# Nine chunks per pass of the attention loop, and half of the k projection before the last y

## The chip, the cores and the metric

The kernel runs on one core of a Trainium2 chip. The metric is device time in microseconds (us) from start to end of the program; the median of several runs counts. The core has five engines that run side by side and wait for each other by semaphores: PE (TensorE, matrix products), DVE (VectorE), ACT (ScalarE), POOL (GpSimd) and SP (SyncE, which issues the DMAs here). Each engine works through its own list of instructions strictly in order.

## What is computed

The reference is one block of a model on x of 2 x 4096 tokens with 512 channels: modulated layer norm, an RWKV-6 attention, a gated residual, a second layer norm and a feed-forward net whose operands are quantised to FP4. The attention, cut to its core:

```python
sx = concatenate([zeros_like(x[:, :1]), x[:, :-1]], axis=1) - x
m = tanh((x + sx * time_maa_x) @ tm_w1).reshape(Bb, Tt, 5, A)
mix = time_maa_wkvrg[None, None] + einsum('btfa,fac->btfc', m, tm_w2)
xw, xk, xv, xr, xg = [x + sx * mix[:, :, i] for i in range(5)]
r, k, v, g = xr @ Wr, xk @ Wk, xv @ Wv, silu(xg @ Wg)
w = exp(-exp(time_decay + tanh(xw @ td_w1) @ td_w2))
def step(state, rkvw):          # over the tokens, for each head
    a = k_t[..., :, None] * v_t[..., None, :]
    y = einsum('bhk,bhkv->bhv', r_t, state + u[None, :, :, None] * a)
    return w_t[..., :, None] * state + a, y
```

Then y is normalised per head, multiplied by g and projected by Wo. Neither the mathematics nor the number of operations is touched by the change.

## The kernel before

The program has two stages, one after the other: `attention` writes x1 to memory, `feed_forward` reads it. Only `attention` is changed.

`attention` cuts the 4096 tokens into 32 chunks of 128 (both sequences together, `ni` = 32) and runs a software pipeline over them. Each engine has a body (`pe_body`, `dve_body`, `act_body`, `pool_body`, `sp_body`), which `run` writes out for iterations 0, 1 and 2, then once inside a hardware loop (`eng.Fori(3, ni - 2)`, iterations 3 to 29, so 27 passes and 26 jumps back), and then for 30 to 33 again. In iteration i a body does three things for three chunks: the projections of chunk i (flag `do_p`), the scan over the tokens of chunk c = i - 1 (`do_w`), and the output projection of chunk f = i - 2 (`do_f`); with `more` it also prepares chunk i + 1.

An iteration has two parts.

- The **scan part**. For each of the 8 sub-blocks n (2 sequences x 4 stretches of 32 tokens) PE computes scores (`pe_scores`, lines 403 to 414, 128 small products in the trace), DVE turns them into the matrix Am and the new state (`dve_A`, L846, L853, L859, L875), and PE multiplies them into y (`pe_y`, L429 and L432, into the bank `YB`). Between them stand the mixing products `pe_delta` (L461), their use on DVE (L743), the decay (L472, L480) and the output projection (L504). The first scores, n = 0, are issued at the very end of the iteration before, so the jump of the loop stands between scores 0 and the first `pe_delta`. The scan ends with `dve_ww` (L755), which copies the decay out of the two banks `PROJ`, then `dve_A` of n = 7, and `pe_y` of n = 7.
- The **tail**. PE transposes the next chunk (`pe_x`, L441), then does the projections k, r (L493), the small product `pe_tm1` (L449), the projections v and g, and the scores 0 of this chunk. A projection fills the two `PROJ` banks half by half (h = 0, 1). Before each half PE waits until the bank's former content is gone: `ww_done` for k, `k_done` for r, `ru_done` for v, `vT_done` for g. ACT copies out k (`act_k`, L611) and r (`act_r`, L615 to L621), and also copies y (`act_yT`, L575), shifts and scales the transposed chunk (`act_hT`, L545, L550) and computes the decay (`act_w`, L597, L600; `act_fg`, L606, L607). DVE computes factors from the decay (L763 to L782), transposes y (L882), makes the token difference (L724, L728), derives scaled k's (L790 to L795) and r's (L806 to L824), transposes v (L828) and k (L833), and ends with the statistics of the chunk after next (L710 to L718).

The order on each engine is that of the bodies as written; no scheduler moves anything. Waits are on semaphore values that depend on the iteration, so in the loop they are made in registers (`after`, `settled_then`).

Of the kernel before, what the change touches and what calls it, by code (L numbers as in the profile page):

```python
# [17 lines left out]


# [1 line left out]

# [68 lines left out]
def after(eng, signal, chunk, k=None):  # L90

    value = signal.at(chunk, k)
    if not isinstance(value, int) or value > 0:
        eng.wait_ge(signal.sem, value)
# [40 lines left out]
def attention(nc, x1, x, maa_x, maa, tm_w1, tm_w2, decay, td_w1, td_w2, faaaa, Wr, Wk, Wv, Wg, Wo,  # L135
              ln_w, ln_b, c_in, wmod, ident_in, diag_in, pick_in, ni=NI):
    with ExitStack() as ctx:
# [5 lines left out]
        def sig(name, per, step=1):  # L143
            return Signal(ctx, nc, name, per, step)
# [195 lines left out]
        ww_done = sig("ww_done", 1)  # L340
# [124 lines left out]
        def xf_wait(eng, i, j):  # L465
            after(eng, xf_done_v, i) if j == 0 else after(eng, xf_done_p, i, j)
# [9 lines left out]
        def pe_td2(pe, i):  # L476
            after(pe, u1_done, i)
            after(pe, mixed, i)
            for g in range(G):
                last = nc.tensor.matmul(PROJ[g // 2][:, (g % 2) * BT:(g % 2 + 1) * BT], w_td2[:, g * P:(g + 1) * P], u1[:],  # L480
                                        start=True, stop=True)
            last.then_inc(td2_done.sem, 1)

        def pe_proj(pe, i, j, free):
            f = ORDER[j]
            xf_wait(pe, i, j)
            buf = xf[:, j % NXF]
            w = {MIX_K: w_k, MIX_R: w_r, MIX_V: w_v, MIX_G: w_g}[f]
            for h in range(2):
                free(h)  # L490
                for g in (2 * h, 2 * h + 1):
                    for k in range(G):
                        last = nc.tensor.matmul(PROJ[h][:, (g % 2) * BT:(g % 2 + 1) * BT], w[:, k, g * P:(g + 1) * P],  # L493
                                                buf[:, k].rearrange("p b t -> p (b t)"), start=(k == 0), stop=(k == G - 1))
                last.then_inc(proj_done.sem, 1)
# [11 lines left out]
        def pe_body(pe, i, do_p, do_w, do_f, more, more2):  # L507
            c, f = i - 1, i - 2
            for n in range(1, 8):
                if n == 1 and do_p:  # L510
                    pe_delta(pe, i, 0)
                if do_w:
                    pe_scores(pe, c, n)
                    pe_y(pe, c, n - 1)
                if n == 2 and do_p:
                    pe_td1(pe, i)
                if 2 <= n <= 5 and do_p:
                    pe_delta(pe, i, n - 1)
                if n == 3 and do_f:
                    pe_wo(pe, f, 0, do_p)  # L520
                if n == 5 and do_f:
                    pe_wo(pe, f, 1, do_p)
                if n == 6 and do_p:
                    pe_td2(pe, i)
            if do_w:
                pe_y(pe, c, 7)
            if more:
                pe_x(pe, i + 1)
            if do_p:
                pe_proj(pe, i, 1, lambda h: after(pe, ww_done, i))  # L530
                pe_proj(pe, i, 2, lambda h: after(pe, k_done, i, h + 1))
            if more:
                pe_tm1(pe, i + 1)
            if do_p:
                pe_proj(pe, i, 3, lambda h: after(pe, ru_done, i, h + 1))
                pe_proj(pe, i, 4, lambda h: after(pe, vT_done, i, h + 1))
                pe_scores(pe, i, 0)
# [34 lines left out]
        def act_yT(act, c, b):  # L572
            after(act, y_done, c, 4 * b + 4)
            after(act, yS_done, c - 1)
            nc.scalar.activation(yT[:, :, b, :], YB[:].rearrange("p (g t) -> p g t", g=G), ACT.Copy).then_inc(yT_done.sem, 1)  # L575
# [19 lines left out]
        def act_w(act, i):  # L595
            after(act, ww_done, i)
            nc.scalar.activation(flat4(wexp), flat4(wexp), ACT.Exp).then_inc(wexp_done.sem, 1)  # L597
            after(act, wexp_done, i)
            after(act, der, i - 1)
            nc.scalar.activation(flat4(wT), flat4(wexp), ACT.Exp, scale=-1.0).then_inc(w_done.sem, 1)  # L600

        def act_fg(act, i):
            after(act, w_done, i)
            after(act, derk, i - 1)
            w4 = wT[:].rearrange("p g b (x e) -> p (g b x) e", e=4)
            nc.scalar.activation(F4[:, :, 1:2], w4[:, :, 0:1], ACT.Copy)  # L606
            nc.scalar.activation(G4[:, :, 2:3], w4[:, :, 3:4], ACT.Copy).then_inc(fg_done.sem, 1)  # L607

        def act_k(act, i, h):
            after(act, proj_done, i, h + 1)  # L610
            nc.scalar.activation(kvar[:, 0, 2 * h:2 * h + 2].rearrange("p g b t -> p (g b t)"), PROJ[h][:], ACT.Copy).then_inc(k_done.sem, 1)  # L611
# [32 lines left out]
        def act_body(act, i, do_p, do_w, do_f, more, more2):  # L644
            c, f = i - 1, i - 2
            if do_p:
                after(act, td1_done, i)
                after(act, td2_done, c)
                nc.scalar.activation(u1[0:D_RANK, :], SMALL[0:D_RANK, 0:BT], ACT.Tanh).then_inc(u1_done.sem, 1)
            if more:  # L650
                act_xn(act, i + 1)
            if do_w:
                act_yT(act, c, 0)
            if do_p:
                act_w(act, i)
            if do_w:
                act_yT(act, c, 1)
            if do_p:
                act_fg(act, i)
            if more:  # L660
                act_hT(act, i + 1)
            if do_w:
                act_square(act, c)
            if do_p:
                act_k(act, i, 0)
                act_k(act, i, 1)
                act_r(act, i, 0)
                act_r(act, i, 1)
                act_k32(act, i)
                act_m1(act, i)  # L670
            if more:
                act_m(act, i + 1)
            if more:
                act_stack(act, i + 1)
            if do_p:
                act_gu(act, i, 0)
                act_gu(act, i, 1)
            if do_w:
                act_affine(act, c)
# [270 lines left out]
        def run(eng, body):  # L950
            body(eng, 0, True, False, False, True, True)
            body(eng, 1, True, True, False, True, True)
            body(eng, 2, True, True, True, True, True)
            with eng.Fori(3, ni - 2) as i:
                body(eng, i, True, True, True, True, True)
            body(eng, ni - 2, True, True, True, True, False)
            body(eng, ni - 1, True, True, True, False, False)
            body(eng, ni, False, True, True, False, False)
            body(eng, ni + 1, False, False, True, False, False)
# [658 lines left out]
```

## Time and profile before

| | us |
|---|---|
| median of 3 runs | 4909.59 |
| lowest, highest | 4905.96, 4915.21 |
| the profiled execution's own time | 4901.52 |
| span from its first to its last instruction | 4899.7 |
| end of the attention in that span, about | 2940 |

The trace lists each instruction with its start and length on its engine, and in square brackets how long the engine sat idle before it and who ended that wait. "issue" as the releaser means that nothing recorded in the profile held the instruction back. Times are from the start of the span. A matrix product in fp32 shows as two records. PE's weight loads are a row of their own, beside PE.

### The profile page before, as it was taken

How to read it: one execution, taken by the hardware profiler on the slowest of the kernel's cores; microseconds unless marked ns; L12 is line 12 of the kernel's file. 1: busy time of each engine (PE TensorE's matmuls, PEld its weight loads, DVE VectorE, ACT ScalarE, POOL GpSimd, SP SyncE). 2: the span in 40 equal slices, each digit the busy share in tenths (PEclk: the TensorE clock that was granted, in tenths of full speed). 3: DMA queues.
4: the chain of work that ended last, by engine and by line, in shares of the span. 5: the costliest groups of instructions: out<-in, count | busy, mean ns of one | idle time of the engine just before them, and what ended most of it. 6: DMA issues, size and time to landing. Idle time of an engine off the chain costs nothing. (4 is left out here: it accounts for less than half of the span.)

```text
span 4899.7 us, 152762 instructions
## 1 busy us (share of the span) xinstructions
PE 4014.8 (82%) x64712; PEld 2745.0 (56%) x64712; DVE 3835.3 (78%) x7929; ACT 1368.0 (28%) x2555; POOL 1387.7 (28%) x735
## 2 busy tenths in 40 slices
PE   5888888888888878888888861499899989989998
PEld 3666666666666766666667651244444444444444
DVE  4676776766767767667677748699999999999997
ACT  2333243332332423323324212212122221212221
POOL 1111211111112111111121113444444444444443
PEclk7888898887988889889889875699999999999999
DMA  3000000000000000000000002001010010101000
GB/s 99 13 27 16 20 24 16 29 16 20 24 16 24 20 16 29 16 20 24 16 25 20 12 24 89 22 20 32 26 32 31 27 32 26 32 26 32 30 28 26
DMA packets 72819, 131.50 MB, mean 27 GB/s; under 512 B 12705, under 2 KB 13473, under 8 KB 72290
## 3 DMA queue, kind: packets, MB, share of 16 engines
q1 hardware_dynamic: 72290, 123.00, 7.9%
q8 instruction: 508, 8.32, 0.7%
q14 instruction: 21, 0.17, 0.0%
HBM read 89.43 MB, written 33.55 MB: 25 GB/s over the span
## 5 line engine op out<-in xcount | busy, mean ns | idle before, releaser
L693 POOL TENSOR_TENSOR xf<-xf,hT 128x1024 f32<-128x1024 f32 x128 | 278.2, 2174 | 1555.1 <-DVE xf L743 1555.1
L859 DVE COPY_PREDICATED Am<-pick,banks 128x64 f32<-128x64 uint8 (+2 forms) x1792 | 460.5, 257 | 121.7 <-DVE Am L859 6.4
L1505 PE MATMUL fbank<-gT,xqT 128*128 128x464 f16 (+1 forms) x2304 | 536.0, 387 | 16.0 <-DVE h L1364 13.8
L1505 PE MATMUL fbank<-uT,xqT 128*128 128x464 f16 (+1 forms) x2304 | 487.7, 361 | 0.0
L1527 PE MATMUL fbank<-dT,hqT 128*128 128x512 f16 x2112 | 476.8, 379 | 0.2 <-ACT hqT L1440 0.2
L704 POOL TENSOR_TENSOR yrs<-yvar,neg_half 128x32 f32<-128x32 f32 x32 | 203.1, 6346 | 789.8 <-DVE yvar L888 789.8
L1505 PEld LDWEIGHTS fbank<-gT,xqT 128*128 128x128 f16 x2304 | 236.6, 104 | 275.8 <-issue 57.0
L1454 ACT ACTIVATE sil<-fbank,und 128x464 f32<-128x464 f32 (+1 forms) x192 | 125.2, 652 | 912.1 <-PE fbank L1505 912.1
L429 PE MATMUL banks<-Am,v_s 32*32 32x32 f32 x8192 | 228.2, 210 | 182.3 <-DVE Am L859 92.2
L1505 PEld LDWEIGHTS fbank<-uT,xqT 128*128 128x128 f16 x2304 | 225.6, 98 | 231.6 <-issue 1.2
L743 DVE SCALAR_TENSOR_TENSOR xf<-banks,col_maa,sx 128x256 f32<-128x256 f32 x640 | 265.0, 477 | 104.2 <-PE banks L461 104.2
L846 DVE TENSOR_TENSOR Am<-banks,diag 128x128 f32<-128x128 f32 x256 | 74.0, 289 | 346.5 <-PE banks L414 344.8
L1321 POOL TENSOR_TENSOR hq<-q16h,s16h 128x1408 f16<-128x1408 f16 x64 | 210.4, 3288 | 443.6 <-DVE s16h L1311 443.6
L1527 PEld LDWEIGHTS fbank<-dT,hqT 128*128 128x128 f16 x2112 | 201.4, 98 | 220.2 <-issue 1.0
L429 PEld LDWEIGHTS banks<-Am,v_s 32*32 32x32 f32 x8192 | 191.6, 121 | 202.7 <-issue 195.6
L403 PE MATMUL banks<-rcol,kvar 32*32 32x80 f32 x8192 | 247.9, 261 | 52.5 <-issue 52.5
L569 ACT ACTIVATE m_stack<-xxx 32x256 fp32r<-32x256 f32 x640 | 265.0, 414 | 75.8 <-DVE xxx L734 58.8
L407 PE MATMUL banks<-rcol,kvar 32*32 32x48 f32 x8192 | 240.5, 223 | 36.3 <-issue 35.9
L403 PEld LDWEIGHTS banks<-rcol,kvar 32*32 32x32 f32 x8192 | 185.6, 121 | 145.2 <-issue 137.2
L853 DVE TENSOR_TENSOR s_tmp<-state,T 128x128 f32<-128x128 f32 x256 | 254.7, 995 | 0.0
L409 PE MATMUL banks<-rcol,kvar 32*32 32x16 f32 x8192 | 226.1, 188 | 33.6 <-issue 33.5
L504 PE MATMUL banks<-w_o,yn 128*128 128x512 f32 x512 | 238.4, 610 | 17.7 <-DVE yn L899 16.9
(230 smaller groups left out, 8995.6 us busy)
## 6 DMA issues: line engine op xcount, KB each, us to landing
x_tok<-in_L_attn_x SPq DMA_DIRECT2D x32, 512.0 KB, 4.0
xres<-in_L_attn_x SPq DMA_DIRECT2D x32, 512.0 KB, 3.9
x_after_attention<-xres SPq DMA_DIRECT2D x32, 512.0 KB, 3.5
xl<-x_after_attention SPq DMA_DIRECT2D x64, 256.0 KB, 2.7
xr<-x_after_attention SPq DMA_DIRECT2D x64, 256.0 KB, 2.7
out<-xr SPq DMA_DIRECT2D x64, 256.0 KB, 2.1
raw_g<-in_L_wmod SPq DMA_DIRECT2D x3, 1024.0 KB, 5.5
raw_g<-in_L_ffn_w_gate SPq DMA_DIRECT2D x1, 2816.0 KB, 10.9
```

Of the source, the lines that this page charges most:

```text
L403: nc.tensor.matmul(sc[d, g * NS:(g + 1) * NS], kvar[d, 0, g, b, 32 * q:32 * q + 32], rcol[d, X, 0:M1], start=True, stop=True)
L407: nc.tensor.matmul(scm[d, g * NM:g * NM + X0 - M1], kvar[d, 1, g, b, 32 * q:32 * q + 32], rcol[d, X, M1:X0], start=True, stop=True)
L409: nc.tensor.matmul(scm[d, g * NM + X0 - M1:(g + 1) * NM], kvar[d, 2, g, b, 32 * q:32 * q + 32], rcol[d, X, X0:SEND], start=True, stop=True)
L429: nc.tensor.matmul(out, v_s[d, g, b, q, :], Am[d, n % 2, g, :], start=True, stop=False)
L504: last = nc.tensor.matmul(SMALL[:], yn[:, k, b, :], w_o[:, b, k, :], start=(k == 0), stop=(k == G - 1))
L569: last = nc.scalar.activation(m_stack[A_RANK * part:A_RANK * (part + 1), j, :], m_part[part % 2][src, f // 4, :], ACT.Copy)
L693: nc.gpsimd.tensor_tensor(xf[:, j % NXF].rearrange("p g b t -> p (g b) t"), xf[:, j % NXF].rearrange("p g b t -> p (g b) t"), hT[:, :, :, ...
L743: last = nc.vector.scalar_tensor_tensor(xf[:, j % NXF, g], PROJ[g // 2][:, (g % 2) * BT:(g % 2 + 1) * BT].rearrange("p (b t) -> p b t", b= ...
L853: nc.vector.tensor_tensor(s_tmp[:], state[:, b, q], t32, ALU.mult).then_inc(s_step.sem, 1)
L859: nc.vector.copy_predicated(dst, mask, src).then_inc((done or A_step).sem, 1)
L1505: last = nc.tensor.matmul(GU[2 * pair + t][:, 0:w], xqT[:, u, a, g, :], W[:, b_, g, lo_:hi_], start=(k == 0), stop=(k == 3 * G - 1))
L1527: last = nc.tensor.matmul(DN[1 - u][:], hqT[:, a, kk, :], dT[:, b_, kk, :], start=(k == 0), stop=(k == 3 * KF - 1))
```

## The change

Three edits.

1. The loop's body now holds nine iterations: `per = gcd(ni - 5, 9)` is 9, and the loop runs 3 times (`lap`) with the iteration number `per * lap + 3 + k`. Two jumps back are left of 26. All five engines are written this way.
2. On PE the first half of the k projection (h = 0) moves from behind `pe_x` to in front of `pe_y(c, 7)`, with its waits: for the mixed input and for `ww_done`.
3. On ACT `act_fg` and the copy of that half, `act_k(i, 0)`, move in front of the second `act_yT`.

```diff
-        def pe_proj(pe, i, j, free):
+        def pe_proj(pe, i, j, free, halves=(0, 1)):
...
-            for h in range(2):
+            for h in halves:
...
+            if do_p:
+                pe_proj(pe, i, 1, lambda h: after(pe, ww_done, i), (0,))
             if do_w:
                 pe_y(pe, c, 7)
             if more:
                 pe_x(pe, i + 1)
             if do_p:
-                pe_proj(pe, i, 1, lambda h: after(pe, ww_done, i))
+                pe_proj(pe, i, 1, lambda h: after(pe, ww_done, i), (1,))
                 pe_proj(pe, i, 2, lambda h: after(pe, k_done, i, h + 1))
...
             if do_p:
                 act_w(act, i)
+            if do_p:
+                act_fg(act, i)
+                act_k(act, i, 0)
             if do_w:
                 act_yT(act, c, 1)
-            if do_p:
-                act_fg(act, i)
             if more:
                 act_hT(act, i + 1)
             if do_w:
                 act_square(act, c)
             if do_p:
-                act_k(act, i, 0)
                 act_k(act, i, 1)
...
-            with eng.Fori(3, ni - 2) as i:
-                body(eng, i, True, True, True, True, True)
+            per = math.gcd(ni - 5, 9)
+            with eng.Fori(0, (ni - 5) // per) as lap:
+                for k in range(per):
+                    body(eng, per * lap + (3 + k), True, True, True, True, True)
```

PE at the end of an iteration in the loop, before: the last of the scores 0, then the loop's count and jump.

```order
L407 MATMUL banks<-rcol,kvar 32x48 x4
L409 MATMUL banks<-rcol,kvar 32x16 x4
L414 MATMUL banks<-v_s,kT 32x32 x16
L954 REGISTER_ALU
L954 COMPARE_AND_BRANCH
```

The same place after, between two of the nine iterations (L462 is the first `pe_delta`).

```order
L410 MATMUL banks<-rcol,kvar 32x16 x4
L415 MATMUL banks<-v_s,kT 32x32 x16
L95 ISA
L462 MATMUL banks<-m_stack,w_tm 128x256 x4
L404 MATMUL banks<-rcol,kvar 32x80 x16
```

The jump is gone; `pe_delta` follows the scores directly.

PE from the last y to the r projection, before (L429 and L432 are the end of y 7, L441 the transposes).

```order
L429 MATMUL banks<-Am,v_s 32x32 x4
L432 MATMUL banks<-r,state 32x32 x4
L94 REGISTER_ALU
L441 MATMUL banks<-ident,xn 128x128 x8
L94 ISA
L493 MATMUL banks<-xf,w_k 128x256 x16
```

The same after; L430 and L433 are the y products, those above L494 of y 6 and those below of y 7.

```order
L433 MATMUL banks<-r,state 32x32 x4
L95 ISA
L494 MATMUL banks<-xf,w_k 128x256 x8
L114 REGISTER_ALU
L430 MATMUL banks<-Am,v_s 32x32 x4
...
L433 MATMUL banks<-r,state 32x32 x4
L95 REGISTER_ALU
L442 MATMUL banks<-ident,xn 128x128 x8
L494 MATMUL banks<-xf,w_k 128x256 x8
```

Eight of the sixteen k products now stand ahead of y 7.

ACT from the decay to the copies of k, before.

```order
L600 ACTIVATE wT<-xxx 128x1024
L94 REGISTER_ALU
L575 ACTIVATE yT<-banks 128x4x128
L94 ISA
L606 ACTIVATE F<-wT 128x256
L607 ACTIVATE G<-wT 128x256
L94 ISA x2
L545 ACTIVATE hT<-hT 128x8
```

The same after.

```order
L603 ACTIVATE wT<-xxx 128x1024
L95 ISA
L609 ACTIVATE F<-wT 128x256
L610 ACTIVATE G<-wT 128x256
L95 ISA
L614 ACTIVATE kvar<-banks 128x512
L95 REGISTER_ALU
L578 ACTIVATE yT<-banks 128x4x128
L95 ISA x2
L548 ACTIVATE hT<-hT 128x8
```

The copy of k's first half, L614, has come in front of the copy of y, L578; the other copy of k stays behind the transposed chunk.

## Rows read from the trace of the kernel before

**Rows 1.** The page, busy time of each engine, share of the span, instructions.

```profile
PE 4014.8 (82%) x64712; PEld 2745.0 (56%) x64712; DVE 3835.3 (78%) x7929; ACT 1368.0 (28%) x2555; POOL 1387.7 (28%) x735
```

**Rows 2.** Windows: stretch, length, busy time by engine, PE clock, DMA share, GB/s.

```profile
387.79:2698.22 2310.43, 1924.34 (x45240) 1540.88 (x45241) 1647.39 (x3953) 771.62 (x1639) 414.75 (x182) 0.87 0.07 21
304.95:387.79 82.84, 73.07 (x1740) 58.84 (x1740) 61.01 (x152) 29.70 (x64) 15.94 (x7) 0.88 0.07 22
220.44:304.95 84.51, 71.82 (x1741) 56.91 (x1742) 61.50 (x153) 29.87 (x64) 15.95 (x7) 0.88 0.07 22
2698.22:2783.43 85.21, 73.88 (x1741) 59.14 (x1742) 59.84 (x146) 29.71 (x64) 15.94 (x7) 0.88 0.05 15
```

**Rows 3.** Timeline of DVE around a jump back: start, us, operation, idle before.

```profile
1541.81 0.29 DVE L846 TENSOR_TENSOR Am<-banks,diag 128x128 f32<-128x128 f32 x1 [2.61 <-PE banks L414]
...
1543.93 0.70 DVE L859 COPY_PREDICATED Am<-pick,banks 128x64 f32<-128x64 uint8 x2
1550.98 0.29 DVE L846 TENSOR_TENSOR Am<-banks,diag 128x128 f32<-128x128 f32 x1 [6.36 <-PE banks L414]
```

**Rows 4.** Timeline of PE around the same jump.

```profile
1541.17 0.45 PE L414 MATMUL banks<-v_s,kT 32*32 32x32 f32 x32
1545.45 0.73 PE L461 MATMUL banks<-m_stack,w_tm 128*128 128x256 f32 x4 [3.82 <-issue]
...
1548.18 1.14 PE L403 MATMUL banks<-rcol,kvar 32*32 32x80 f32 x26 [1.66 <-issue]
```

**Rows 5.** Waits of PE from 387.7 to 2698.3: total us, times, longest.

```profile
PE banks L461 <- issue: 103.1, 26, 4.4
```

**Rows 6.** Timeline of DVE at two iteration starts without a jump.

```profile
223.88 0.29 DVE L846 TENSOR_TENSOR Am<-banks,diag 128x128 f32<-128x128 f32 x1 [0.99 <-PE banks L414]
...
225.70 0.62 DVE L859 COPY_PREDICATED Am<-pick,banks 128x64 f32<-128x64 uint8 x2
...
304.95 0.29 DVE L846 TENSOR_TENSOR Am<-banks,diag 128x128 f32<-128x128 f32 x1 [2.69 <-PE banks L414]
...
307.65 0.29 DVE L846 TENSOR_TENSOR Am<-banks,diag 128x128 f32<-128x128 f32 x1
```

**Rows 7.** DMA queues, 387 to 476, then 300 to 387: packets, MB, share.

```profile
q8 instruction: 16, 0.26, 1.2%
...
q8 instruction: 14, 0.23, 1.2%
q14 instruction: 3, 0.02, 0.1%
```

**Rows 8.** Timeline of PE in a tail, from the last y.

```profile
1501.15 0.24 PE L432 MATMUL banks<-r,state 32*32 32x32 f32 x6
1505.21 0.57 PE L429 MATMUL banks<-Am,v_s 32*32 32x32 f32 x7 [3.82 <-DVE Am L859]
...
1508.28 7.28 PE L493 MATMUL banks<-xf,w_k 128*128 128x256 f32 x32
1515.39 7.07 PE L493 MATMUL banks<-xf,w_r 128*128 128x256 f32 x32
```

**Rows 9.** Timeline of DVE in the same tail.

```profile
1500.99 1.21 DVE L755 TENSOR_SCALAR xxx<-banks 128x1024 f32<-128x1024 f32 x1
...
1512.67 1.67 DVE L728 SCALAR_TENSOR_TENSOR xxx<-sx,col_maax,hT 128x256 f32<-128x256 f32 x4
1516.22 1.23 DVE L790 TENSOR_TENSOR kvar<-kvar,G 128x1024 f32<-128x1024 f32 x1 [1.88 <-ACT kvar L611]
```

**Rows 10.** Windows of the same tail, columns as in rows 2.

```profile
1506.00:1508.00 2.00, 2.00 (x48) 1.94 (x39) 1.90 (x5) 1.38 (x3) 0.00 (x0) 0.50 0.70 247
1508.00:1541.70 33.70, 33.62 (x275) 28.33 (x273) 23.80 (x42) 22.19 (x53) 6.35 (x1) 0.99 0.01 1
```

**Rows 11.** Timelines of PE and DVE in the second iteration written out.

```profile
252.73 5.22 PE L504 MATMUL banks<-w_o,yn 128*128 128x512 f32 x8
...
259.57 0.29 DVE L846 TENSOR_TENSOR Am<-banks,diag 128x128 f32<-128x128 f32 x1 [4.27 <-PE banks L414]
```

More of the change, by code:

```diff
@@ L20 @@
 from contextlib import ExitStack
+import math
 import concourse.bass as bass
```

## The prediction

> **What bounds the kernel now.** The page comes first. Over the span PE is busy 82% and DVE 78% [rows 1], so neither is full and the two take turns waiting. The change touches only the attention, so I looked for the length of one of its iterations. I took the start of `dve_A` of n = 0 (L846) as the mark. From the first start after a jump to the first start behind the loop are 26 iterations: 2310.43 / 26 = 88.86 us each [rows 2]. Three further iterations of the same shape have no jump ahead of their scan: the first pass of the loop, 82.84 us, and two that are written out, 84.51 and 85.21 us [rows 2]. The reader sees here already that an iteration behind a jump costs 3.7 to 6.0 us more.
>
> The timelines show where. In the loop DVE starts `dve_A` of n = 0 at 1541.81, is done with it at 1544.63, and then sits idle 6.36 us until the scores of n = 1 arrive at 1550.98 [rows 3]. From mark to mark that is 9.17 us. PE had ended the scores 0 at 1541.62 and stood still 3.82 us before the next product and 1.66 us more among the scores, both for "issue", nothing that the profile shows as a semaphore [rows 4]. Not one case but all: 26 such stops before L461, together 103.1 us, 4.0 each [rows 5]. The instruction queue of PE agrees: 16 blocks were fetched in an iteration behind a jump, 14 in the one without [rows 7]. Without a jump the same distance from n = 0 to n = 1 is 307.65 - 304.95 = 2.70 us, or 223.88 - 220.44 = 3.44 us [rows 2, 6].
>
> The tail is bound by PE. It is busy 33.62 of 33.70 us, at a clock of 0.99 [rows 10]. Right before that stretch it stands idle 3.82 us, because y 7 waits for Am of n = 7 [rows 8]. DVE then waits for what PE makes: 1.88 us for k [rows 9], and at the tail's end 2.61 us for scores 0 [rows 3].
>
> **Edit 1, nine iterations a pass.** It removes 24 of 26 jumps. From the rows the gross gain at one boundary is 9.17 - 2.70 = 6.47 us. Part is given back, since the scan that follows without a jump is not as smooth: whole iterations without one are only 6.0, 4.4 and 3.7 us shorter than 88.86 [rows 2]. One reason is visible: in the second of them the output projection L504 took 5.22 us, and DVE waited 4.27 us for the scores behind it [rows 11]. The first pass of the loop, 82.84, is the one that has exactly the loop's code, with waits made in registers; the other two have constants there. So the sum takes 5.0 us, between the 6.0 of the exact code and the mean 4.1 of the other two: 24 x 5.0 = 120 us. The high bound is the whole gap, 24 x 6.47 = 155 us. The low bound is an estimate: a `dve_A` in a written-out iteration took 226.32 - 223.88 = 2.44 us [rows 6] against 1544.63 - 1541.81 = 2.82 in the loop [rows 3], since its waits are made with constants. Eight times 0.38 is 3.0 of the 4.1, so 1.1 would be left, 24 x 1.1 = 26 us. The bodies have no more register steps than before (79 for each iteration on DVE by the order of the instructions, 82 before), so no wait becomes dearer.
>
> On what causes such a stop the Trainium skill bears ("Runtime: NRT & Kernel Launch", section "Instruction fetch mechanics"). It says that a taken branch to a target outside the fetched window waits for a DMA of the target, and that streaming straight code is mostly hidden. By the first statement the trace agrees, with 4.0 us a jump. By the second the full 155 us would be gained; the 84.51 and 85.21 speak against taking it whole. Another page ("Advanced Engine Details and Errata", section "Control Flow Timing") puts a compare-and-branch at about 108 ns; by it alone 24 jumps would be worth 2.6 us, which the 3.82 us stops contradict.
>
> **Edit 2, half of the k projection ahead of y 7.** PE stops at 1501.39 and `ww_done` comes at 1502.20 [rows 8, 9]. The half costs 7.28 / 2 = 3.64 us and ends at 1505.84 instead of leaving PE idle until 1505.21. So y 7 starts 0.63 us late. y 7 and the transposes take 1508.28 - 1505.21 = 3.07, to 1508.91; the other half takes 3.64, to 1512.55. Before, k ended at 1515.39, when r began [rows 8]. Everything behind it on PE comes 2.84 us earlier, if nothing else becomes late.
>
> What could be late next? DVE's token difference waits for the transposes, 0.63 us later now, so `xxx`, which ended at 1512.67 + 1.67 = 1514.34, ends at 1514.97 at the latest [rows 9]. PE wants it for `pe_tm1`, which now comes at 1519.6: 4.6 us to spare. DVE's k work can start at once, since k was ready for it 1516.22 - 1515.39 = 0.83 us after PE's end of k [rows 8, 9], which makes 1513.38; the 1.88 us of waiting vanishes and DVE is 1.25 us ahead of before. It then meets r, 2.84 us ahead, where it is 1.6 us behind PE's gain; before, it waited there too, so at most 0.4 us of that shows, and each later wait of DVE in the tail was for PE too. At the end it had 2.61 us in hand [rows 3]. So PE still sets the end. The saving counts in iterations 1 to 31, the ones with both a scan and projections: 31 x 2.8 = 87 us. In iteration 0 there is no y 7 and nothing is won.
>
> Bounds: y 7 and the transposes ran at a clock of 0.50 after the idle time [rows 10]. If the half fills that gap and the clock stays up, up to 0.8 us more is won, 3.6 in all, or 112 us. If instead the half itself runs at half clock, it takes 7.28, y 7 starts at 1509.5 and k ends at 1516.2, which is 0.8 us later than before: a loss of 25 us. PE works until 1501.39 at full length just before [rows 8], so the value near full clock is taken.
>
> **Edit 3, ACT's order.** `act_fg` needs nothing but the decay. It fills ACT's wait for y 7 and costs nothing. The copy of k's first half costs 0.83 us at most, by the same difference as above; it waits for PE's half at 1505.84 and ends at 1506.67, while y 7 starts at 1505.84 and is the next thing ACT waits for. So it hides too, but for a few tenths. If the half is slow, the copy of y waits behind it, but y 7 on PE stands behind the same half, so no new delay arises.
>
> **The sum.** 4901.5 - 120 - 87 = 4694.5 for an execution like the profiled one. The median of the runs shown lies 8.1 us above that execution, so 4702.6; I give 4702.
>
> **Rivals.**
> - *Streaming gives most back.* Nine different iterations lie at other block boundaries and other phases of the clock, and stops like that of rows 11 take most of the gain: 26 + 87 = 113 us, time 4797. For it: 85.21. Against: the first pass, 82.84.
> - *The tail gains nothing.* The half runs at low clock, or DVE becomes the one that is waited for. The gain is 120 us, time 4790. For it: the 0.50 [rows 10]. Against: DVE's 2.61 us in hand.
> - *All of it.* Straight code streams without a stop and the clock stays up: 155 + 112 = 267 us, time 4643. The Trainium skill's "mostly hidden" (the page and section named above) would give this side of it, the 155.
> - *Slower.* Before, the short lists of DVE, ACT and POOL stay inside and are not fetched again in the loop; the queue q14 moved 3 blocks in the first pass and none in the next window [rows 7]. Now DVE streams as well. If DVE itself stops for a block, nothing covers it in the scan, where each step hangs on it. At 4.0 us a stop as for PE, two in an iteration, 8.0, cost what both edits bring (5.0 + 2.8), and from there on the change loses. Three in each of 24 give 24 x (12.0 - 7.8) = 100 us, 5010. Against it: the iterations written out already stream on DVE, and all of DVE's waits there end with PE or ACT.
> - *Nothing happens* would need the loop to jump as often as before. The instruction order rules that out, with nine bodies between two jumps.
>
> **How the numbers follow.** Forecast 0.70, streaming gives back 0.12, tail gains nothing 0.09, all of it 0.05, slower 0.03, nothing measurable 0.01. The range runs from just above the full gain to just beyond the two weak cases, 4650 to 4805. It leaves out the full gain, the slower case and nothing, about 0.09, and about as much again for sizes beyond the bounds. A change within 0.2% (10 us) is about what a measurement of this kernel cannot tell from none. Faster 0.96, same 0.01, slower 0.03.
>
> **What would show it.** In the trace after: from mark to mark 88.9 - 5.0 - 2.8, about 81 us within a lap, and 86 behind the two jumps left. The stops before the first `pe_delta` gone but for two. Fourteen blocks for PE in an iteration. The idle time before y 7 near 0.8 us and in front of the half, not behind it. From `ww_done` to the next `dve_A` of n = 0 36.8 us instead of 1541.81 - 1502.20 = 39.6. DVE still idle before scores 0. I am wrong if DVE shows stops for issue, if the whole scan has PE stops of 2 to 3 us that DVE waits for, or if the half of k takes 7 us.

## The result and the profile after

The changed kernel takes 4743.6 us (median of 4 runs, 4739.1 to 4748.5) against 4912.4 us before; the ratio is 0.9658, 95% interval 0.9641 to 0.9675. That is 169 us less, where 207 were forecast. The profiled execution has a span of 4739.7 us against 4899.7, so 160.0 us less, and its parts say where they come from.

The page of the kernel after, busy time as in [rows 1]:

```profile
PE 3970.0 (84%) x64712; PEld 2691.6 (57%) x64712; DVE 3788.9 (80%) x7929; ACT 1375.0 (29%) x2555; POOL 1388.1 (29%) x735
```

The windows of the kernel after. The first row is the 26 iterations that answer to the first of [rows 2]; the second is one tail that ran well (in the first pass of the loop, ahead of the 26), the third one that did not.

```profile
383.87:2548.83 2164.96, 1888.05 (x45240) 1497.98 (x45240) 1597.15 (x3952) 778.16 (x1639) 411.68 (x182) 0.89 0.07 22
348.53:383.87 35.34, 35.11 (x345) 29.55 (x346) 28.66 (x59) 26.18 (x57) 6.35 (x1) 1.00 0.10 30
1421.84:1463.55 41.71, 38.45 (x409) 32.11 (x410) 28.84 (x58) 25.95 (x57) 6.35 (x1) 0.92 0.08 25
```

The 26 iterations went from 2310.4 to 2165.0 us, which is 145.5 of the 160.0. One iteration is 83.27 us long on the mean instead of 88.86. The rest is in the iterations ahead of them, about 4 us, and in those written out behind the loop, about 11, which have the moved half of k too. The feed-forward stage did not change: from the last output of the attention on DVE to the end it is 1964 us in both.

The boundary between two iterations, timeline of DVE after (compare [rows 3]):

```profile
383.87 0.29 DVE L849 TENSOR_TENSOR Am<-banks,diag 128x128 f32<-128x128 f32 x1 [2.50 <-PE banks L415]
...
386.76 0.29 DVE L849 TENSOR_TENSOR Am<-banks,diag 128x128 f32<-128x128 f32 x1
```

and of PE (compare [rows 4]):

```profile
383.35 0.45 PE L415 MATMUL banks<-v_s,kT 32*32 32x32 f32 x32
383.73 0.75 PE L462 MATMUL banks<-m_stack,w_tm 128*128 128x256 f32 x4
```

`pe_delta` follows the scores with no stop, and DVE goes from n = 0 to n = 1 in 2.89 us instead of 9.17. The waits of PE over the 26 iterations (compare [rows 5]):

```profile
PE banks L433 <- issue: 86.6, 48, 3.6
PE banks L430 <- issue: 60.1, 35, 3.3
...
PE banks L462 <- issue: 7.4, 2, 3.7
```

Two lines of the same view before, both for the y products:

```profile
PE banks L429 <- DVE Am L859: 83.0, 28, 3.8
PE banks L429 <- issue: 71.9, 69, 2.6
```

The stops before the first `pe_delta` are gone but for two, those of the two jumps left. But others have appeared: PE now stops inside the y products (L430, L433), 147 us in all. Before, L429, the same line as L430 here, had 72 us of them and L432 none. The first of the two lines is the gap ahead of y 7 that edit 2 was to fill, 3.2 us an iteration; after, PE waits for Am only 2.5 us in all.

The tail that ran well, timeline of PE (compare [rows 8]):

```profile
348.76 3.81 PE L494 MATMUL banks<-xf,w_k 128*128 128x256 f32 x16 [0.95 <-DVE xxx L758]
352.50 0.26 PE L430 MATMUL banks<-Am,v_s 32*32 32x32 f32 x8
...
353.20 1.07 PE L442 MATMUL banks<-ident,xn 128*128 128x128 f32 x8
354.11 3.62 PE L494 MATMUL banks<-xf,w_k 128*128 128x256 f32 x16
357.57 7.07 PE L494 MATMUL banks<-xf,w_r 128*128 128x256 f32 x32
```

The half of k stands in the former gap; PE idles 0.95 us ahead of it and not at all behind. From the start of y 7 to the second half of k it takes 1.61 us instead of 3.07, at a clock of 1.00, where it was 0.50 before [rows 10]. This stretch is as short in all of the 26 iterations. The idle time ahead of the half is not: there PE waits for the decay only once, 0.5 us. Otherwise it arrives late, since it has stood for issue before, and the half starts 2.3 us after the decay is copied out on the mean. The tail that ran badly, the same engine:

```profile
1425.70 0.26 PE L430 MATMUL banks<-Am,v_s 32*32 32x32 f32 x2 [3.25 <-issue]
1426.05 6.20 PE L494 MATMUL banks<-xf,w_k 128*128 128x256 f32 x16
1432.88 1.07 PE L442 MATMUL banks<-ident,xn 128*128 128x128 f32 x8
```

Here PE stopped 3.25 us for issue inside y 6, after which the half of k ran at low clock and took 6.20 us. The clock from 1426.05 to 1432.25 was 0.59. The tail is 41.71 us long, longer than any of the 26 in the kernel before. Over the 26 the half takes 4.75 us on the mean, 3.7 in eight of them and 6.2 to 6.5 in five, and the tails last from 35.6 to 41.7 us.

To see where an iteration gained and lost I took, for each kernel, the starts of the eight `dve_A` (the line L846 or L849) of the 26 iterations, and averaged the distances. All tables below are made that way.

| us, mean of 26 iterations | before | after | difference |
|---|---|---|---|
| n = 0 to 1 (behind the jump) | 9.57 | 3.80 | -5.77 |
| n = 1 to 7 (the scan) | 39.24 | 41.74 | +2.50 |
| n = 7 to the next 0 (the tail) | 40.05 | 37.73 | -2.32 |
| iteration | 88.86 | 83.27 | -5.59 |

The first and the last row of differences came about as forecast in kind. The middle one is the surprise: the scan gives back 2.5 us an iteration, 65 us in all. Most of it is in two steps: n = 5 to 6 takes 8.31 us instead of 6.16, and n = 3 to 4 takes 7.27 instead of 6.44. From n = 1 to 7 DVE now stands idle 8.3 us an iteration instead of 4.0, nearly always for PE, while its own work there takes 30.3 us instead of 32.1; why the latter is less stays open.

### The profile page after: what moved, and what is told of

Read it like the earlier page. It is cut to its first block and busy times, and to the rows that moved or that the text cites. A ratio compares the mean times of both kernels' runs of the same rounds, so it can differ in the third digit from the quotient of the medians.

```text
span 4739.7 us, 152203 instructions
## 1 busy us (share of the span) xinstructions
PE 3970.0 (84%) x64712; PEld 2691.6 (57%) x64712; DVE 3788.9 (80%) x7929; ACT 1375.0 (29%) x2555; POOL 1388.1 (29%) x735
## 5 line engine op out<-in xcount | busy, mean ns | idle before, releaser
L433 PE MATMUL banks<-r,state 32*32 32x32 f32 x8192 | 212.5, 204 | 103.8 <-issue 103.8
L849 DVE TENSOR_TENSOR Am<-banks,diag 128x128 f32<-128x128 f32 x256 | 74.1, 290 | 278.0 <-PE banks L415 276.6
L505 PE MATMUL banks<-w_o,yn 128*128 128x512 f32 x512 | 262.9, 662 | 21.4 <-DVE yn L902 16.9
L430 PE MATMUL banks<-Am,v_s 32*32 32x32 f32 x8192 | 209.0, 205 | 75.9 <-issue 69.9
L494 PE MATMUL banks<-xf,w_k 128*128 128x256 f32 x1024 | 266.0, 418 | 7.4 <-issue 4.5
L1494 PE MATMUL fbank<-ident,hq 128*128 128x128 f16 x1408 | 121.8, 247 | 150.1 <-POOL hq L1326 112.9
L408 PE MATMUL banks<-rcol,kvar 32*32 32x48 f32 x8192 | 219.1, 215 | 33.2 <-issue 33.1
L404 PE MATMUL banks<-rcol,kvar 32*32 32x80 f32 x8192 | 221.6, 246 | 28.4 <-issue 28.4
L410 PE MATMUL banks<-rcol,kvar 32*32 32x16 f32 x8192 | 208.5, 183 | 40.3 <-issue 40.3
```

The costliest lines, as they stand in the source:

```text
L404: nc.tensor.matmul(sc[d, g * NS:(g + 1) * NS], kvar[d, 0, g, b, 32 * q:32 * q + 32], rcol[d, X, 0:M1], start=True, stop=True)
L408: nc.tensor.matmul(scm[d, g * NM:g * NM + X0 - M1], kvar[d, 1, g, b, 32 * q:32 * q + 32], rcol[d, X, M1:X0], start=True, stop=True)
L433: last = nc.tensor.matmul(out, state[d, b, q, g, :], r32[d, X, :], start=False, stop=True)
L505: last = nc.tensor.matmul(SMALL[:], yn[:, k, b, :], w_o[:, b, k, :], start=(k == 0), stop=(k == G - 1))
```

## The experiments

### The two edits apart

`e1_unroll` is the changed kernel with the order of PE and ACT as before, so nine iterations a pass alone. The part of PE is shown; ACT's is that of `e3_act_old` below.

```diff
-            if do_p:
-                pe_proj(pe, i, 1, lambda h: after(pe, ww_done, i), (0,))
             if do_w:
                 pe_y(pe, c, 7)
             if more:
                 pe_x(pe, i + 1)
             if do_p:
-                pe_proj(pe, i, 1, lambda h: after(pe, ww_done, i), (1,))
+                pe_proj(pe, i, 1, lambda h: after(pe, ww_done, i))
```

> Nine iterations per pass, the k projection and ACT's order as before. Theory A (the two edits add up; the scan gives back 2.5 us an iteration because PE's instructions stream, whatever the tail does): the 24 jumps bring 6.2 us each at the start of the scan, minus 2.5 us in it, so 24 x 3.7 = 89 us, time 4823. The sum from n = 1 to n = 7 is about 41.7 us as in the changed kernel, against 39.2 before. Theory B (what is given back comes with the moved half of k, which shifts where PE's clock is low): the unrolling alone keeps 5.0 us or more per jump, time 4790 or less, and the stretch from n = 1 to n = 7 stays near 40 us.

`e2_khalf` is the changed kernel with one iteration a pass.

```diff
-            per = math.gcd(ni - 5, 9)
+            per = 1
```

> One iteration per pass as before, with the moved half of k and ACT's new order. Theory A (edits add up): the gain is the rest of the 169 us, some 75 to 80 us, time 4835; the tail is 37.5 us against 40.05. Theory B (the half brings its 2.8 us or more in every iteration and the loss lies in the combination): 31 x 2.8 = 87 us or more, time 4825 or less, tail 37 or less in every iteration, as the clock finds the same pattern each time.

| | us | ratio to before (95%) | n 0 to 1 | scan | tail | iteration |
|---|---|---|---|---|---|---|
| before | 4909.9 | | 9.57 | 39.24 | 40.05 | 88.86 |
| e1_unroll | 4828.2 | 0.9824 (0.9804 to 0.9844) | 3.88 | 42.17 | 39.92 | 85.98 |
| e2_khalf | 4825.6 | 0.9835 (0.9809 to 0.9860) | 9.62 | 39.42 | 37.07 | 86.11 |
| after | 4743.6 | 0.9658 (0.9641 to 0.9675) | 3.80 | 41.74 | 37.73 | 83.27 |

The edits add up: 82 + 84 = 166 us, against 169 together, within the intervals. The whole loss in the scan, 2.9 us, is there in `e1_unroll` without the moved half; in `e2_khalf` the scan is as before. There Theory A stands. In `e2_khalf` itself the time and the mean tail are nearer to what Theory B gave (4825 us and 37) than to Theory A's 4835 and 37.5, but not "in every iteration": its tails range from 35.8 to 39.8 us. So, as means of the 26 iterations, the unrolling brings 5.7 us at the boundary and pays 2.9 back. For each of the 24 jumps removed that is 3.1 us net by the 26 iterations of the trace (75 us), and 82 / 24 = 3.4 us by the medians. The moved half brings 3.0 us a tail on its own and 2.2 beside the unrolling.

### What ACT's order is worth

`e3_act_old` is the changed kernel with ACT as before: copy of y, then `act_fg`, then the transposed chunk, and only then both copies of k.

```diff
-            if do_p:
-                act_fg(act, i)
-                act_k(act, i, 0)
             if do_w:
                 act_yT(act, c, 1)
+            if do_p:
+                act_fg(act, i)
             if more:
                 act_hT(act, i + 1)
             if do_w:
                 act_square(act, c)
             if do_p:
+                act_k(act, i, 0)
                 act_k(act, i, 1)
```

> Nine iterations per pass and the half of k on PE ahead of y 7, but ACT's order as before (copy of y, then the decay factors, then both copies of k). If ACT's order hides as the prediction said, the time is that of the changed kernel within 10 us: the first copy of k is wanted only by r, 3.6 us later. If the order on ACT is needed, r waits for the copy of k behind the transposed chunk (about 358 instead of 353 in the trace, when k's second half ends at 357.6), up to 1 us an iteration, 30 us slower.

It took 4808.9 us (0.9784, 0.9763 to 0.9805), 65 us slower than the changed kernel. Its trace is of the longest of its four runs, 4827.9 us. The waits of PE over the 26 iterations:

```profile
PE banks L494 <- ACT kvar L614: 46.8, 26, 1.8
```

In every iteration the r projection stands 1.8 us, because its bank still holds the first half of k, which ACT copies only behind the transposed chunk. The tail is 40.04 us instead of 37.73, as long as before the change. I had expected at most 30 us. With it PE never waits for the copy of k, as the prediction said, but without it the edit on PE brings only about 20 us (4828.2 to 4808.9).

### The jumps left, and the length of a pass

`e4_per27` and `e5_per3` change one number each.

```diff
-            per = math.gcd(ni - 5, 9)
+            per = 27
```

> All 27 iterations in one pass, so no jump back at all; otherwise the changed kernel. If each jump costs what the two left show (8.83 and 9.31 us from n = 0 to n = 1 instead of 3.35), 2 x 5.7 = 11 us less, 4732, minus up to 5 us given back in the scan: 4732 to 4737. If a long stretch of code streams worse (its instructions are fetched once and never again), it is the same or slower than 4744.

```diff
-            per = math.gcd(ni - 5, 9)
+            per = 3
```

> Three iterations per pass: nine passes and eight jumps instead of two. By the run with the unrolling alone a jump removed is worth 82 / 24 = 3.4 us net, so six more cost 20 us: 4764. If instead the first few removed jumps bring most (the streaming loss grows with the length of the pass), it stays within 8 us of 4744.

With no jump at all it took 4748.3 us (0.9663, 0.9645 to 0.9682), the same as the changed kernel, where 7 to 12 us less were expected. Its trace shows where they went. The 26 iterations take 2155.1 us instead of 2165.0, so the last two jumps did bring 10 us. But the three iterations behind the loop, from n = 0 of the first to n = 7 of the last, take 209.7 us instead of 193.3, with the same code. With eight jumps it took 4790.8 us (0.9771, 0.9740 to 0.9803), 47 us more than with two, where I expected 20. Its timeline of DVE around a jump:

```profile
556.04 0.29 DVE L849 TENSOR_TENSOR Am<-banks,diag 128x128 f32<-128x128 f32 x1 [2.99 <-PE banks L415]
...
566.67 0.29 DVE L849 TENSOR_TENSOR Am<-banks,diag 128x128 f32<-128x128 f32 x1 [7.82 <-PE banks L415]
```

Of its 26 iterations the 8 behind a jump take 87.2 us and the other 18 take 83.0, so a jump costs 4.2 us net here; six of them are 25 us. The 26 iterations together took 2192.1 us, 27.1 more than after. The remaining 14 us of the spans' difference (4780.8 against 4739.7) are in the iterations ahead of the loop and behind it, whose code is the same in both: the three behind it take 203.4 us here and 193.3 in the changed kernel. `e2_khalf` and `e4_per27` have that code too and take 202.6 and 209.7, so the changed kernel's 193.3 is the exception, worth 9 to 16 us in its favour. Comparisons of nearly equal kernels by their total time turn on it. What sets it stays open; that it is the phase in which the code meets the clock and the instruction blocks is a guess.

### Is it the number of instructions, or PE's time?

The stops for issue in the scan suggest that PE waits for its instructions, of which a product in fp32 needs four: the trace shows two matmul records and two weight loads for each. (The "128 small products" of `pe_scores` named above are such matmul records, of 64 products.) Three runs change their number. `e6_dup_scan` issues the last 16 products of `pe_scores` twice for n = 2 to 5.

```diff
-            for g in range(G):
+            for g_ in range(2 * G if 2 <= n <= 5 else G):
+                g = g_ % G
                 for d in HEADS:
                     last = nc.tensor.matmul(sc[d, G * NS + g * K:G * NS + (g + 1) * K], kT[d, g, b, q, :], v_s[d, g, b, q, :], start=True, stop=True)
```

> The changed kernel with 16 small products (kT by v_s, the 32 x 32 ones behind each scores) issued twice for n = 2 to 5, with the same result: 256 more PE instructions in the scan of each iteration, one instruction block of 16 KB more, 4 x 0.45 = 1.8 us of PE time. Theory F (in the scan PE is held by the arrival of its instructions, about 3.8 us for each block): up to 3.8 us more an iteration, clearly more than the next run, 31 x 3 = 90 us or more. Theory C (only PE's own time and its clock count): most of the 1.8 us hides under DVE, 0 to 30 us slower than the changed kernel.

`e7_dup_tail` has the same edit with `5 * G if n == 0 else G`.

> The same 64 extra products an iteration, but all behind the scores of n = 0, at the end of the tail, where the rows show no block fetched for 20 us. PE's time there is on the path: 1.8 us an iteration, 32 x 1.8 = 58 us slower than the changed kernel under both theories. Theory F: less than the run with the extra products in the scan costs, or the same if the block that is drained here is missing at the scan's start. Theory C: more than the run in the scan, since nothing hides it here.

`e9_fewer` leaves the products L410 out for n = 2 to 5, so part of the scores is stale.

```diff
-                for d in HEADS:
+                for d in (() if 2 <= n <= 5 else HEADS):
                     nc.tensor.matmul(scm[d, g * NM + X0 - M1:(g + 1) * NM], kvar[d, 2, g, b, 32 * q:32 * q + 32], rcol[d, X, X0:SEND], start=True, stop=True)
```

> The changed kernel without the 16 products of 32 x 16 (L410) for n = 2 to 5; their columns of the scores are left stale, so part of the attention's result is missing. 256 PE instructions less in the scan, one block of 16 KB less, and about 4 x 0.3 us of PE time. Theory F: PE's stops in the scan (8 to 9 us an iteration for issue) shrink by 2 us or more and the iteration by 1 to 2, 30 to 60 us faster. Theory C: the iteration follows PE's own time at most, 0 to 20 us faster.

And two controls add time on PE with few instructions. `e10_time_scan`:

```diff
         def pe_wo(pe, f, b, fenced):
...
+            for _ in range(2 - b):
+                nc.tensor.matmul(SMALL[:], yn[:, 0, b, :], w_o[:, b, 0, :], start=True, stop=True)
```

> Control to the run with extra products in the scan: the changed kernel with three long products added (the first product of the output projection repeated, twice for b = 0 at n = 3 and once for b = 1 at n = 5, with the same result). By the rows 3 x 0.6 = 1.8 us of PE time at full clock as there, but 12 instructions instead of 256. Theory F (what counts in the scan is the number of PE instructions): much less than the 148 us there, 0 to 60 us slower than 4744. Theory C (PE's time): like that run, 100 us or more.

`e11_time_tail`:

```diff
         def pe_proj(pe, i, j, free, halves=(0, 1)):
...
+                for _ in range(4 if (j, h) == (4, 1) else 0):
+                    nc.tensor.matmul(PROJ[h][:, 0:BT], w[:, 0, 2 * h * P:(2 * h + 1) * P],
+                                     buf[:, 0].rearrange("p b t -> p (b t)"), start=True, stop=True)
```

> Control to the run with extra products in the tail: four products of the g projection repeated in each iteration, 4 x 0.455 = 1.8 us of PE time with 16 instructions instead of 256. PE's time is on the path there: 32 x 1.8 = 58 us under both theories. Theory F: the 119 us of the run with 256 short ones had some 60 us for their instructions. Theory C: 119 us here too.

The second control has the length that it was meant to have, 4 x 0.455 us. The first does not. The 0.6 us of its expectation are one of a product's two records. Four products of the output projection take 3.60 us at a clock of 1.00, so one takes 0.90, and three add 2.7 us and not 1.8:

```profile
500.19 3.60 PE L507 MATMUL banks<-w_o,yn 128*128 128x512 f32 x8
```

In the 26 iterations the added products, two records each, were busy 91.06 us on PE (first column behind the length), 3.50 us an iteration:

```profile
396.41:2638.08 2241.67, 91.06 (x156) 29.97 (x156) 0.90 0.07 21
```

| against after, 4743.6 us | added for an iteration | us | ratio to before (95%) | difference |
|---|---|---|---|---|
| e6_dup_scan | 256 instructions, 1.8 us of PE, in the scan | 4891.9 | 0.9967 (0.9954 to 0.9979) | +148 |
| e10_time_scan | 12 instructions, 2.7 us, in the scan | 4858.2 | 0.9891 (0.9859 to 0.9924) | +115 |
| e7_dup_tail | 256 instructions, 1.8 us, in the tail | 4863.0 | 0.9908 (0.9884 to 0.9931) | +119 |
| e11_time_tail | 16 instructions, 1.8 us, in the tail | 4808.6 | 0.9802 (0.9777 to 0.9828) | +65 |
| e9_fewer | 256 instructions less in the scan | 4649.7 | 0.9463 (0.9446 to 0.9479) | -94 |

Since the low clock stretches what is added, the windows of the 26 iterations compare better. In the order of the table (the changed kernel's row stands above), busy time of PE first:

```profile
395.82:2678.70 2282.88, 1960.51 (x48568) 1557.42 (x48569) 1541.48 (x3953) 778.01 (x1639) 411.46 (x182) 0.87 0.07 21
396.41:2638.08 2241.67, 1954.57 (x45397) 1524.20 (x45397) 1562.51 (x3953) 778.65 (x1639) 411.62 (x182) 0.90 0.07 21
403.90:2658.26 2254.36, 1949.52 (x48568) 1554.69 (x48568) 1597.17 (x3952) 777.75 (x1638) 411.92 (x182) 0.88 0.07 21
393.28:2595.58 2202.30, 1930.08 (x45449) 1532.91 (x45449) 1607.54 (x3952) 778.81 (x1639) 412.01 (x182) 0.90 0.07 22
380.72:2472.14 2091.42, 1854.37 (x41912) 1463.16 (x41913) 1541.23 (x3952) 779.08 (x1639) 415.92 (x182) 0.89 0.07 23
```

| us, mean of 26 iterations | iteration | PE busy | PE idle | idle against after |
|---|---|---|---|---|
| after | 83.27 | 72.62 | 10.65 | |
| e6_dup_scan, 256 more | 87.80 | 75.40 | 12.40 | +1.75 |
| e10_time_scan, 12 more | 86.22 | 75.18 | 11.04 | +0.39 |
| e7_dup_tail, 256 more | 86.71 | 74.98 | 11.73 | +1.08 |
| e11_time_tail, 16 more | 84.70 | 74.23 | 10.47 | -0.18 |
| e9_fewer, 256 less | 80.44 | 71.32 | 9.12 | -1.53 |

The last column is the answer. Each difference in it is uncertain by some 0.4 us, from the scatter of the single iterations. The number of instructions counts by itself: 256 more or less move PE's idle time by 1.1 to 1.75 us an iteration the same way, and long products leave it within that uncertainty. In the tail the medians say so too: time alone costs 65 us for 32 x 1.8 = 58, the same length in 256 instructions, at another place of the tail, 54 us more, 1.7 us an iteration. That is so although no block is fetched there for 20 us; the tail's mean of PE's stops for issue rose from 1.1 to 2.6 us. Whether the instructions come late, or PE takes so many short ones only at some rate, these runs do not separate.

PE's own time counts as well, also in the scan, and there each theory was wrong once. Theory F had put the long products at 60 us at most; they cost 115, as Theory C had it (100 or more), and the iteration grew by 2.95 us where PE's busy time grew by 2.56. Theory C had put the short ones of `e6_dup_scan` at 30 at most, since most would hide under DVE; they cost 148. And `e9_fewer` gained 94 us, more than either had. How the 148 us divide the medians do not say, as the two runs add different lengths at different places: the long products stand in front of the output projection's own, which scores wait for.

The windows of the output projection alone (L504) show how the clock bears on the scan, here in the kernel before, columns as in [rows 2] but for PE and its weight loads only:

```profile
387.79:2698.22 2310.43, 187.20 (x416) 75.66 (x416) 0.87 0.07 21
```

The same in the kernel after (L505):

```profile
383.87:2548.83 2164.96, 212.41 (x416) 86.34 (x416) 0.89 0.07 22
```

The same 416 records, two for each of 208 products, take 212.4 us instead of 187.2, 1.0 us an iteration more, though the clock over the whole stretch is higher (0.89 against 0.87). In the kernel before, the low clock lay in the steps behind the jump: of 23.9 us at the low level in an iteration, 17.9 were between n = 0 and n = 3, and 0.2 between n = 5 and 6. After, it is 17.9 us in all, but 2.9 of them between n = 5 and 6, right where the scores that DVE waits for stand behind L505. The step from n = 5 to 6 is 2.15 us longer than before.

### Moving the output projection out of the way

`e8_wo_late` puts its second half behind the scores of n = 6.

```diff
-                if n == 5 and do_f:
+                if n == 6 and do_f:
                     pe_wo(pe, f, 1, do_p)
```

> The changed kernel with the second half of the output projection (L505, b = 1) moved behind the scores of n = 6 and y 5, so that the scores 6 no longer stand behind it. From n = 5 to n = 6 the changed kernel takes 8.3 us against 6.2 in the kernel before. If it is the output projection at low clock that the scores wait for, this falls to about 6.4 and n = 6 to 7 grows by 0.5 to 1.5, net 0.5 to 1.5 us an iteration, 15 to 40 us faster than 4744. If the stretch is long because of missing instructions, the time moves less than 10 us.

`e12_wo_last` puts it behind n = 7, in front of the moved half of k, and its use on DVE behind the last `dve_A`.

```diff
-                if n == 5 and do_f:
+                if n == 7 and do_f:
                     pe_wo(pe, f, 1, do_p)
...
-                if n == 6 and do_f:
+                if n == 7 and do_f:
                     dve_out(dve, f, 1)
```

> The changed kernel with the second half of the output projection (b = 1) behind the scores of n = 7 and y 6, in front of the moved half of k, and DVE's use of it behind its n = 7. In the changed kernel PE idles about 0.9 us there for the decay, and the scores 6 stand behind that product. If the scan's loss from n = 5 to n = 7 (14.5 us against 12.1) goes with it and the tail grows only by the 1.5 us that don't fit into the idle time, 0.5 to 2 us an iteration, 15 to 60 us faster than 4744. If PE is short as a whole from n = 5 to the scores 0, the time only moves and stays within 10 us, as it did one place earlier.

| | us | ratio to before (95%) | n 5 to 6 | n 6 to 7 | tail | iteration |
|---|---|---|---|---|---|---|
| after | 4743.6 | 0.9658 (0.9641 to 0.9675) | 8.31 | 6.16 | 37.73 | 83.27 |
| e8_wo_late | 4743.6 | 0.9661 (0.9632 to 0.9691) | 6.01 | 9.53 | 36.85 | 83.06 |
| e12_wo_last | 4789.0 | 0.9761 (0.9736 to 0.9785) | 6.03 | 6.83 | 40.70 | 84.25 |

The step n = 5 to 6 falls to 6.0 us in both, so it was the output projection that the scores waited for. But in `e8_wo_late` the next step takes it all back. In `e12_wo_last` the tail pays 3.0 us, more than the 1.9 won in the scan. The waits of DVE of that kernel:

```profile
DVE Am L849 <- PE banks L415: 160.3, 107, 6.7
DVE xres L912 <- PE banks L505: 80.3, 26, 5.3
```

DVE now stands 3.1 us in each iteration for the output projection itself, in front of its own tail. It was the wrong place: DVE's copy-out is in order too. No version tried that does all of the work beats the changed kernel by its total time.

## Why the prediction held, and which term was off

**Direction, range and edit 2 were right.** The tail was bound by PE, and the half of k goes into the gap. Alone it brought 84 us where 31 x 2.8 = 87 were put down. That this is so near is luck in part, since two terms were off and cancelled. In `e2_khalf` the half took 5.28 us on the mean and not 3.64, 1.16 of them stops inside it. And y 7 with the transposes took 1.6 us and not 3.07 at the higher clock, so 1.5 us were won there, where the bound put at most 0.8. What would be late next was right: nothing that sets the end, as long as ACT's order comes along. DVE does now wait 27 us in all for ACT's copy of y, which it did not before, but it still idles 2.1 us or more before every scores 0, 2.50 on the mean.

**Edit 1 was mis-sized.** The gross term was right: 6.47 us forecast at the boundary, 5.7 measured as a mean that includes the two jumps left, which is 6.2 for each jump removed. The step that failed is "the sum takes 5.0 us, between the 6.0 of the exact code and the mean 4.1 of the other two". It allowed 1.5 us of loss in the scan; `e1_unroll` showed 2.9, so the net is 3.1 to 3.4 us and the term 75 to 82 us, not 120. By the medians that is 38 us, as much as the whole miss. The first pass of the loop, 82.84 us, was a single iteration and a lucky one, trusted because it had the loop's code. In `e1_unroll`, the run with the same tail, the 24 iterations without a jump ahead range from 82.4 to 89.4 us, with a mean of 85.7; the two written-out iterations, 84.51 and 85.21, were nearer. The truth lay between the low bound of 1.1 us and that mean of 4.1.

**The rivals.** "Streaming gives most back" was the nearest, by its mechanism if not its size. "The tail gains nothing", by a half of k at low clock, came in five of 26 tails (clock 0.57 to 0.59, tails of 40.5 us and more). "Slower", by DVE stopping for its own instructions, did not happen, though q14, the queue that the prediction took for the short lists, now moves 91 blocks in the 26 iterations against one before. The instruction queues of one iteration after, 465 to 548 (compare [rows 7]):

```profile
q8 instruction: 14, 0.23, 1.1%
q14 instruction: 4, 0.03, 0.1%
```

PE's 14 blocks are as forecast. DVE's waits for issue over the 26 iterations stay under 1 us in all for each line. On the rule weighed ahead ("Runtime: NRT & Kernel Launch" in the Trainium skill, section "Instruction fetch mechanics"): that a jump makes an engine wait for its code, the runs confirm. That streaming is mostly hidden holds for DVE here and not for PE, whose stops for issue fell only from 11.3 to 10.3 us an iteration when nearly all the jumps went.

**The signs.** Forecast for an iteration within a lap was about 81 us, measured 83.1; behind the two jumps 86, measured 87.4 and 83.9. From `ww_done` to the next `dve_A` of n = 0 36.8 us were forecast for a tail that took 39.6; the means are 38.4 after and 40.1 before. The idle time of 0.8 us ahead of the half is there in `e2_khalf`, where it reaches 0.95, and hardly in the changed kernel. Of the three signs of being wrong one came: the scan has PE stops of 2 to 3 us that DVE waits for. Besides those at jumps there are 38 stops of 2 us or more in the 26 iterations, 9 before, and DVE's idle time in the scan doubled. The half of k never took 7 us in the changed kernel, but up to 6.5.

**What stays open.** The scan's loss, 2.5 us in the changed kernel, has two visible parts: PE's stops for issue from n = 1 to 7 are 2.5 us an iteration longer (5.5 before, 8.0 after), and the output projection runs 1.0 us longer, with more low clock where it stands. They overlap, and may be linked: the low clock of [rows 10] came right behind a stand of 3.82 us. No run here holds one fixed while the other changes. How far each is the cause is argued, not shown.

## What to carry to other kernels

A hardware loop's jump can be priced from the trace in two steps: the gap behind it, and what the straight code then loses elsewhere; take whole iterations for the second, several of them, and not the best one. Where an engine runs hundreds of very short instructions, removing jumps moves its waiting for instructions rather than ending it, and here about half of the gain was paid back. When work is pulled into a gap on one engine, the copy that frees its output must be pulled forward on the other engine as well: without that, 65 of the 84 us that the move brings were gone. And a control has to be measured too: the length of what it adds is read from its own trace, since one product can be several records.

## What the hardware showed that I had not expected

- 256 short PE instructions cost more than their time: PE's idle time moved by 1.1 to 1.75 us an iteration, in the scan and in the tail. In the tail this is so even at the end of a stretch in which no instruction block had been fetched for 20 us, 54 us over the kernel.
- PE time added to the scan did not hide under DVE, although PE is not busy without a break there: the iteration grew by 2.95 us for 2.56 us more of busy PE, and in the tail by 1.44 for 1.62.
- Less low clock is not always better. After the change PE was at the low level 17.9 us an iteration instead of 23.9, but at a place where a product stood on the path.
- The same written-out iterations behind the loop took 193.3 us in the changed kernel and 202.6 to 209.7 in three others.
